# A graph network's second edge ranking moved from a stage of its own into the edge-score loop of the first layer

## The chip, the cores and the metric

The kernel runs on one core of a Trainium2 chip. The metric is the device time of one execution, in microseconds (us). Engines: PE is TensorE (matrix products; PEld its weight loads), DVE is VectorE, ACT is ScalarE, POOL is GpSimd, SP is SyncE, which here only issues DMAs. Each engine runs its own instruction stream in order; streams meet at semaphores.

## What is computed

Two layers, each a graph network and then a feed-forward network, on 3,125 nodes of 256 values and 53,125 edges sorted by destination. The parts that matter here, in short:

```python
# layer 0, graph: scores of the edges, softmax over each destination, weighted sum
h  = LN(x) @ Wn.T + bn
a  = leaky_relu(sum((h[src] + edge_attr @ We.T + be) * attn), 0.01)
x += relu(segment_sum(h[src] * softmax_by_dst(a), dst))
x += experts0(LN(x))                     # layer 0, feed-forward, 8 experts, top 2
# layer 1, graph: a second aggregation, now into the edges' SOURCE nodes
s   = LN(x) @ W
x += relu(batchnorm(segment_sum(edge_weight * s[dst], src) + bias))
...                                      # layer 1, feed-forward, with a third edge list
```

The second aggregation sums into `src`, by which the edges are not sorted. The kernel therefore ranks the edges by source: it computes for every edge the slot it has in an order by source tile (128 nodes), each tile padded to whole blocks of 6 x 128 slots. It then scatters one record per edge (destination, lane of the source, weight) to those slots in DRAM.

## The kernel before

The edges stand as 128 partitions x 416 chunks; the nodes are 25 tiles of 128. `build_kernel` emits blocks one after the other. Each block is a program for every engine, and the next begins when all engines have finished it. The blocks that matter, in order:

1. setup, layer norm and projection of layer 0, and `emit_sort_edges` (the third edge list's ranks; PE, VectorE and ScalarE).
2. **`emit_edge_scores`** (tiles `es_...`). A loop of 8 turns with two pieces each makes 16 pieces of 26 chunks. SP loads for a piece the transposed edge attributes `es_ea` (1,664 KB) and the source lanes `es_lane` (832 KB) into one of two buffers, once `read` says that the piece two before is done with. PE multiplies 26 f32 columns (L389, each counted in `step`), then makes 78 products with the one-hot lanes (L394; the last one counts `mm`). VectorE builds the one-hot lanes (L359, `hot`), waits for `mm`, and picks, reduces and adds the scores (L363 to L369), then counts `read`. POOL issues 176 scatters of the third edge list's records (L967). They are paced by single events: before each, `pace` waits for a count of `step` on PE.
3. `emit_aggregate` "a0": the first aggregation.
4. **`emit_rank_edges`** (tiles `se_...`), the stage that the change removes. POOL fills a record array with the values for empty slots (L1015 to L1018), and SP writes it to DRAM (L1010). VectorE makes a one-hot of all edges against all 25 source tiles (L1049). Then, per tile, PE makes two products over 416 columns (L1025: rank within a chunk, L1026: counts per chunk), and VectorE turns them into positions (L1053 to L1070). VectorE lets PE go on to the next tile with `tile_read`. L1072 to L1084 put the positions into `rece` and the tiles' ends into `eranges`.
5. layer norm and projection "l1", the gate, and `emit_experts` "f0". There POOL scatters the rest of the third list's records and, with `rece`, the 416 chunks of the second aggregation.
6. the second aggregation "a1" and the rest.

The wait that keeps PE and VectorE together in a tile of the ranking is this:

```python
with pe.Fori(0, NT) as t:
    pe.wait_ge(tile_read, t + 1)
    ...matmul(psr...); matmul(pst...).then_inc(ranked, 1)
# VectorE, per tile:
v.wait_ge(ranked, t + 1)
...scan, subtract, add (reads psr, pst)
v.drain().then_inc(tile_read, 1)
...multiply by the one-hot, add to pos and blocks
```

## Time and profile before

| what | us |
|---|---|
| median of 3 runs (3980.2 to 3986.33) | 3983.19 |
| the profiled execution | 3978.59 |
| its span, first to last instruction | 3976.6 |
| PE busy in the span | 2652.6 (67%) |
| VectorE busy | 1509.7 (38%) |
| ScalarE busy | 759.2 (19%) |
| POOL busy | 1882.4 (47%) |
| mean granted TensorE clock, share of full speed | 0.708 |

The profiled execution is one run on the chip. The shares are averages over stages that follow each other, and each stage has an engine of its own that sets its length. So the table tells what the whole is made of, and not what an edit in one stage is worth. A timeline row gives the start, the duration, engine, line and operation, output <- inputs and, in brackets, the idle time before it with what ended it. `x52` on such a row means that so many equal instructions were merged. An f32 product of PE runs as two passes, so the 26 columns of L389 are 52 records. A name with q (SPq, DVEq) is the engine's sequencer or queue.

### The profile page before, as it was taken

Reading aid. Unit: us, or ns where it says so; the run is one execution under the profiler, and the core shown is the slowest. Engines: PE = TensorE matmul, PEld = TensorE weight load, DVE = VectorE, ACT = ScalarE, POOL = GpSimd, SP = SyncE. Lnnn points to the kernel's source line nnn. Section 1 sums busy time; section 2 is a strip of 40 time slices with the busy share of each in tenths; the row PEclk is TensorE's granted clock in tenths of the full one; section 3 lists DMA queues with packets and bytes.
Section 4 is the critical chain, followed back from the end, with each engine's and each line's share of the span. In section 5 each row is a group of like instructions: output and inputs, shape, how many; then the busy total and the mean of one; then the engine's idle time right before and its main releaser. Section 6 shows DMA issues by size and latency. Waiting matters only on the chain. (4 is left out here: it accounts for less than half of the span.)

```text
span 3976.6 us, 46896 instructions
## 1 busy us (share of the span) xinstructions
PE 2652.6 (67%) x10550; PEld 1812.6 (46%) x10551; DVE 1509.7 (38%) x3668; ACT 759.2 (19%) x2605; POOL 1882.4 (47%) x1926
## 2 busy tenths in 40 slices
PE   3259886566666661389999999577776663989810
PEld 2135776333333330266676777333333343666600
DVE  5864112656666548622222222322222224001075
ACT  0136000232222220122222222111111111222200
POOL 0000664556565650056666666166666620666602
PEclk9555555666666665589999999766666665999955
DMA  2012442222232330010000000133333311111001
GB/s 71 26 44 65 149 160 104 69 76 79 75 80 75 80 76 13 0 32 11 12 12 12 12 13 1 60 90 89 91 89 91 90 44 26 18 14 19 8 36 35
DMA packets 125070, 213.67 MB, mean 54 GB/s; under 512 B 56130, under 2 KB 83095, under 8 KB 122711
## 3 DMA queue, kind: packets, MB, share of 16 engines
q0 software_dynamic: 75808, 125.28, 12.8%
q1 hardware_dynamic: 49206, 87.79, 6.5%
q8 instruction: 18, 0.29, 0.0%
q14 instruction: 38, 0.30, 0.0%
HBM read 197.42 MB, written 15.52 MB: 54 GB/s over the span
## 5 line engine op out<-in xcount | busy, mean ns | idle before, releaser
L503 POOL DMA_INDIRECT a0rows<-table,a0idx x462 | 472.4, 1022 | 349.6 <-ACT a0idx L488 235.3
L967 POOL DMA_INDIRECT records<-k_recg x288 | 287.4, 998 | 724.5 <-ACTq L306 366.6
L503 POOL DMA_INDIRECT a1rows<-table,a1idx x444 | 420.4, 947 | 316.8 <-ACT a1idx L488 172.1
L533 PE MATMUL a1ps<-a1rows,a1w 128*128 128x256 f32 x888 | 414.0, 590 | 195.3 <-DMA a1rows<-table,a1idx 135.3
L533 PE MATMUL a0ps<-a0rows,a0w 128*128 128x257 f32 x924 | 437.5, 614 | 154.2 <-ACT a0w L703 93.0
L967 POOL DMA_INDIRECT erecords<-k_rece x416 | 404.3, 972 | 209.0 <-issue 98.1
L795 PE MATMUL f0up<-k_xnT,f0w 128*128 x1280 | 380.3, 453 | 54.4 <-ACT f0hid L827 30.6
L1396 POOL DMA_INDIRECT gt_land<-table_gat,gt_source x281 | 266.0, 947 | 293.5 <-DVEq L1425 144.1
L533 PEld LDWEIGHTS a0ps<-a0rows,a0w 128*128 128x128 f32 x924 | 239.0, 292 | 348.5 <-issue 161.9
L533 PEld LDWEIGHTS a1ps<-a1rows,a1w 128*128 128x128 f32 x888 | 209.1, 274 | 400.2 <-issue 283.9
L805 PE MATMUL f0dn<-f0w,f0hid 128*128 128x256 f32 x1600 | 357.8, 380 | 11.4 <-issue 10.7
L805 PEld LDWEIGHTS f0dn<-f0w,f0hid 128*128 128x128 f32 x1600 | 303.4, 190 | 57.5 <-issue 16.9
L795 PEld LDWEIGHTS f0up<-k_xnT,f0w 128*128 128x128 f32 x1280 | 243.5, 196 | 187.6 <-issue 54.4
L746 DVE SCALAR_TENSOR_TENSOR k_x<-f0dn,k_gate,k_x 128x256 f32 (+1 forms) x200 | 87.0, 479 | 507.8 <-PE f0dn L805 312.4
L827 ACT ACTIVATE f0hid<-f0up,f0b1now 128x384 f32<-128x384 f32 (+1 forms) x320 | 168.0, 527 | 526.1 <-PE f0up L795 351.0
L572 DVE TENSOR_SCALAR a1w<-k_iota,k_elane,k_eweight 128x128 f32<-128x128 f32 x444 | 145.9, 366 | 267.3 <-PE a1ps L533 167.9
L1623 PE MATMUL f1up<-k_xnT,gt_arena 128*128 x640 | 190.5, 454 | 27.7 <-DVE gt_arena L1440 13.5
L1633 PE MATMUL f1dn<-gt_arena 128*128 128x256 f32 x800 | 189.3, 388 | 26.3 <-issue 22.9
L389 PE MATMUL es_ps<-k_we_attn,es_ea 128*128 128x1 f32 x832 | 180.7, 349 | 20.6 <-DMA es_lane<-lane_row 14.2
L488 ACT COPY a1idx<-k_esource 128x1 int32 x444 | 82.8, 191 | 580.4 <-PE a1ps L533 369.8
L389 PEld LDWEIGHTS es_ps<-k_we_attn,es_ea 128*128 128x128 f32 x832 | 180.0, 331 | 21.6 <-DMA es_lane<-lane_row 14.4
L703 ACT ACTIVATE a0w<-a0nb,k_score 128x128 f32 x462 | 143.5, 388 | 233.2 <-DVE a0nb L640 186.8
(389 smaller groups left out, 3115.2 us busy)
## 6 DMA issues: line engine op xcount, KB each, us to landing
es_ea<-in_eaT SPq DMA_DIRECT2D x16, 1664.0 KB
es_lane<-lane_row SPq DMA_DIRECT2D x16, 832.0 KB
so_rowl<-glane_row SPq DMA_DIRECT2D x32, 256.0 KB
a0rows<-table,a0idx POOLq DMA_INDIRECT x462
a1rows<-table,a1idx POOLq DMA_INDIRECT x444
erecords<-k_rece POOLq DMA_INDIRECT x416
table<-k_tbl SPq DMA_DIRECT2D x10, 650.0 KB, 3.4
records<-k_recg POOLq DMA_INDIRECT x288
```

Source lines behind the costliest of these rows:

```text
L389: nc.tensor.matmul(ps[i][:, 2, c:c + 1], ea[:, i, c * P:(c + 1) * P], S.we_attn[:, 0:1], start=True, stop=True).then_inc(step, 1)
L503: pool.indirect_dma_start(rows[:, i, 0:TW], None, table, bass.IndirectOffsetOnAxis(ap=idx[:, i:i + 1], axis=0)).then_inc(gathered[i], 16)
L533: nc.tensor.matmul(sum_of(t), w[:, i, :], rows[:, i, 0:width], start=False, stop=False).then_inc(agg_done, 1)
L572: nc.vector.tensor_scalar(w[:, i, :], S.iota[:, 0:P], S.elane[:, bass.ds(c + i, 1)], S.eweight[:, bass.ds(c + i, 1)], ALU.is_equal, ALU.mu ...
L703: nc.scalar.activation(w[:, i, :], nb[:, bass.ds(g % RING, 1), i, :].rearrange("p a n -> p (a n)"), ACT.Exp, bias=S.score[:, bass.ds(c + i ...
L795: ins = nc.tensor.matmul(up[q % 2][:, 0:size], w1[:, k, m * P:(m + 1) * P], S.xnT[:, k, bass.ds(g * (U * P) + a * P, size)], start=(k == 0 ...
L805: ins = nc.tensor.matmul(down[j][:, 0:D], hid[half][:, k, (j - a) * P:(j - a + 1) * P], w2[:, k, :], start=(k == 0), stop=(k == KH - 1))
L827: nc.scalar.activation(hid[half][:, m, :], up[q % 2][:, 0:(b - a) * P], ACT.Gelu, bias=bias_now[:, m:m + 1]).then_inc(hid_ready, 1)
L967: pool.indirect_dma_start(self.rec_dram, bass.IndirectOffsetOnAxis(ap=self.rec[:, c + 1, 0:1], axis=0), self.rec[:, c + 1, 1:R], None).the ...
L1396: pool.indirect_dma_start(land[:, j, :], None, S.table_gat, bass.IndirectOffsetOnAxis(ap=source[:, j:j + 1], axis=0)).then_inc(gathered[la ...
L1623: ins = nc.tensor.matmul(up[q % 2][:, 0:size], w1[:, k, m * P:(m + 1) * P], S.xnT[:, k, bass.ds(g * (U * P) + a * P, size)], start=(k == 0 ...
L1633: ins = nc.tensor.matmul(down[j][:, 0:D], hid[half][:, k, (j - a) * P:(j - a + 1) * P], w2[:, k, :], start=(k == 0), stop=(k == KH - 1))
```

## The change

The block `emit_rank_edges` is gone, and with it its call in front of "l1". `emit_edge_scores` gets its work:

- **Start of the block.** POOL's three memsets of the empty records come before its scatters (now into `erec_sb`, which is free until the scattered records are read back). SP waits for them and issues the 855 KB write to DRAM ahead of its first loads. VectorE makes the 25-tile one-hot (now `tile_hot`) before its loop, and PE waits for that (`hots`) before anything else. The two loads of the node numbers and two integer steps are gone, and four other short steps come behind the one-hot, since setup has left the same values in `S.srct`, `S.dstf` and `S.src`.
- **The loop.** Each turn of two pieces takes three tiles: 24 in 8 turns. PE does a tile's two products ahead of piece 0, one ahead of piece 1, and one between piece 1's f32 columns and its one-hot products. VectorE does one tile behind piece 0's one-hot and two behind piece 1's, both ahead of its wait for `mm`.
- **After the loop.** Tile 24, then the steps that write `eranges` and `rece`, ahead of the score's last steps.

The pacing of the scatters is as before. `rece` now lives with the edges' tiles, and the first table's tiles are given up before the sort, to make room. (The tables of setup, `emit_aggregate` and the experts are not touched.)

```diff
--- before.py
+++ after.py
@@ -311,12 +311,25 @@
...
+        pos, incl, part, zero = (sb(n, [P, NC], F32) for n in ("pos", "incl", "part", "zero"))
+        posi, lanei = sb("posi", [P, NC], I32), sb("lanei", [P, NC], I32)
+        tile_hot = sb("tilehot", [P, NT, NC], BF16)
+        trib, onesb = sb("trib", [P, P], BF16), sb("onesb", [P, P], BF16)
+        blocks, base, cnt = (sb(n, [P, 1], F32) for n in ("blocks", "base", "cnt"))
+        starts, under = sb("starts", [P, KB], F32), sb("under", [P, KB], F32)
+        row = sb("row", [P, NT + 1], F32)
         ps = [ctx.enter_context(nc.psum_tensor(f"es_ps{i}", [P, 3, 512], F32)) for i in range(2)]
+        psr = ctx.enter_context(nc.psum_tensor("es_psr", [P, 512], F32))
+        pst = ctx.enter_context(nc.psum_tensor("es_pst", [P, 512], F32))
+        hots, ranked, tile_read, filled, emptied = (sem("es_" + n) for n in ("hots", "rank", "tread", "fill", "empty"))
+        GB = BG * P
         block = ctx.enter_context(nc.Block())
         lane_row = S.lane_row.rearrange("(a n) -> a n", a=1)
...
         @block.sync
         def _(sp):
+            sp.wait_ge(filled, 1)
+            sp.dma_start(rec_dram.rearrange("(p c) r -> p c r", p=P), S.erec_sb[:]).then_inc(emptied, 16)
             with sp.Fori(0, NPIECE // 2) as o:
                 for i in range(2):
                     sp.wait_ge(read, 2 * o + i + 1)
@@ -325,10 +338,14 @@
...
+            sp.wait_ge(emptied, 16)
             scatter.finish(sp)
 
         @block.gpsimd
         def _(pool):
+            nc.gpsimd.memset(S.erec_sb[:, :, 0:1], 0)
+            nc.gpsimd.memset(S.erec_sb[:, :, 2:3], 0)
+            nc.gpsimd.memset(S.erec_sb[:, :, 1:2], 2 * P).then_inc(filled, 1)
...
@@ -353,11 +370,52 @@
...
+
+            v.sem_inc(tile_read, 1)
+            nc.vector.tensor_copy(trib[:], S.tri[:])
+            nc.vector.tensor_copy(onesb[:], S.ones[:, 0:P])
+            nc.vector.memset(zero[:], 0.0)
+            nc.vector.memset(pos[:], 0.0)
+            nc.vector.memset(blocks[:], 0.0)
+            nc.vector.memset(row[:], 0.0)
+            nc.vector.tensor_scalar(starts[:], S.iota[:, 0:KB], float(GB), None, ALU.mult)
+            nc.vector.tensor_tensor(tile_hot[:], S.srct[:, 0:NC].unsqueeze(1).to_broadcast([P, NT, NC]),
+                                    S.iota[:, 0:NT].unsqueeze(2).to_broadcast([P, NT, NC]), ALU.is_equal)
+            v.drain().then_inc(hots, 1)
+            nc.vector.tensor_scalar(lanei[:], S.src[:, 0:NC], P - 1, None, ALU.bitwise_and)
+            nc.vector.tensor_copy(rec[:, 1:NC + 1, 1], S.dstf[:, 0:NC])
+            nc.vector.tensor_copy(rec[:, 1:NC + 1, 3].bitcast(F32), S.ew[:, 0:NC])
+            v.drain()
+            nc.vector.tensor_copy(rec[:, 1:NC + 1, 2], lanei[:])
+
+            def rank_tile(t):
+                nc.vector.tensor_scalar(base[:], blocks[:], float(GB), None, ALU.mult)
+                v.wait_ge(ranked, t + 1)
+                nc.vector.tensor_tensor_scan(incl[:], pst[:, 0:NC], zero[:], 0.0, ALU.add, ALU.add)
+                v.drain()
+                nc.vector.tensor_tensor(part[:], incl[:], pst[:, 0:NC], ALU.subtract)
+                nc.vector.tensor_scalar(under[:], starts[:], incl[:, NC - 1:NC], None, ALU.is_lt)
+                v.drain()
+                nc.vector.tensor_tensor(part[:], part[:], psr[:, 0:NC], ALU.add)
+                nc.vector.tensor_reduce(cnt[:], under[:], AX.X, ALU.add)
+                v.drain().then_inc(tile_read, 1)
+                nc.vector.scalar_tensor_tensor(part[:], part[:], base[:, 0:1], tile_hot[:, bass.ds(t, 1), :].rearrange("p a c -> p (a c)"),
+                                               ALU.add, ALU.mult)
+                nc.vector.tensor_scalar(cnt[:], cnt[:], 1.0, None, ALU.max)
+                v.drain()
+                nc.vector.tensor_tensor(pos[:], pos[:], part[:], ALU.add)
+                nc.vector.tensor_tensor(blocks[:], blocks[:], cnt[:], ALU.add)
+                v.drain()
+                nc.vector.tensor_copy(row[:, bass.ds(t + 1, 1)], blocks[:])
+
             with v.Fori(0, NPIECE // 2) as o:
                 for i in range(2):
                     v.wait_ge(arrived[i], 32 * o + 32)
                     nc.vector.tensor_scalar(onehot[:, i, :], lane[:, i, :], S.lane[:, 0:1], None, ALU.is_equal
                                             ).then_inc(hot, 1)
+                    rank_tile(o * 3 + i)
+                    if i == 1:
+                        rank_tile(o * 3 + 2)
                     v.wait_ge(mm, 2 * o + i + 1)
...
@@ -369,6 +427,22 @@
...
                     v.drain().then_inc(read, 1)
+            with v.Fori(NT - 1, NT) as t:
+                rank_tile(t)
+            v.drain()
+            nc.vector.tensor_copy(S.eranges[:], row[:])
+            nc.vector.tensor_copy(posi[:], pos[:])
+            v.drain()
+            nc.vector.tensor_scalar(lanei[:], posi[:], P - 1, None, ALU.bitwise_and)
+            v.drain()
+            nc.vector.tensor_scalar(posi[:], posi[:], 7, None, ALU.logical_shift_right)
+            nc.vector.tensor_copy(part[:], lanei[:])
+            v.drain()
+            nc.vector.tensor_copy(pos[:], posi[:])
+            v.drain()
+            nc.vector.scalar_tensor_tensor(part[:], part[:], float(ES), pos[:], ALU.mult, ALU.add)
+            v.drain()
+            nc.vector.tensor_copy(rec[:, 1:NC + 1, 0], part[:])
...
@@ -380,14 +454,24 @@
...
         def _(pe):
+            def rank_tile(t):
+                pe.wait_ge(tile_read, t + 1)
+                counts = tile_hot[:, bass.ds(t, 1), :].rearrange("p a c -> p (a c)")
+                nc.tensor.matmul(psr[:, 0:NC], trib[:], counts, start=True, stop=True)
+                nc.tensor.matmul(pst[:, 0:NC], onesb[:], counts, start=True, stop=True).then_inc(ranked, 1)
+
             pe.wait_ge(split, 1)
+            pe.wait_ge(hots, 1)
             with pe.Fori(0, NPIECE // 2) as o:
                 for i in range(2):
+                    rank_tile(o * 3 + i)
                     pe.wait_ge(read, 2 * o + i + 1)
                     pe.wait_ge(arrived[i], 32 * o + 32)
                     for c in range(PIECE):
                         nc.tensor.matmul(ps[i][:, 2, c:c + 1], ea[:, i, c * P:(c + 1) * P], S.we_attn[:, 0:1],
                                          start=True, stop=True).then_inc(step, 1)
+                    if i == 1:
+                        rank_tile(o * 3 + 2)
                     pe.wait_ge(hot, 2 * o + i + 1)
                     for c in range(PIECE):
...
@@ -395,6 +479,8 @@
...
                         ins.then_inc(step if c < PIECE - 1 else mm, 1)
+            with pe.Fori(NT - 1, NT) as t:
+                rank_tile(t)
...
@@ -1691,37 +1668,35 @@
...
+        rece = sb_edges("rece", [P, NC + 1, 4], I32)
...
-            emit_layernorm_project(nc, S, "l0", S.w_aug, D + 1, False, rows_and_score, table, S.table_sb)
+            with ExitStack() as inner:
+                S.table_sb = sb("tbl0", [P, NT, TW], F32, inner)
+                S.w_aug = sb("w_aug", [P, KD, D + 4], F32, inner)
+                S.bn_row = sb("bn_row", [P, D], F32, inner)
+                emit_setup(nc, S, A)
+
...
+                emit_layernorm_project(nc, S, "l0", S.w_aug, D + 1, False, rows_and_score, table, S.table_sb)
             emit_sort_edges(nc, S, A)
-            emit_edge_scores(nc, S, A, Scatter(nc, S, "sa", recg, rec_dram, 0, EARLY))
+            emit_edge_scores(nc, S, A, Scatter(nc, S, "sa", recg, rec_dram, 0, EARLY), rece, erec_dram)
         emit_aggregate(nc, S, "a0", table, True)
...
         with ExitStack() as stage:
...
-            emit_rank_edges(nc, S, "se", NC, BG, A["dst_pc"][:, 0:NC], A["src_pc"][:, 0:NC], S.ew[:, 0:NC], ES, rece, erec_dram,
-                            S.eranges)
...
```

The deleted function is the one printed above.

On **PE**, the body of the edge-score loop before:

```order
L384 ISA
L387 ISA
L389 MATMUL es_ps<-k_we_attn,es_ea 128x1 x26
L394 MATMUL es_ps<-es_parts,es_hot 128x25 x78
L386 REGISTER_ALU
L389 MATMUL es_ps<-k_we_attn,es_ea 128x1 x26
L394 MATMUL es_ps<-es_parts,es_hot 128x25 x78
L384 REGISTER_ALU
L384 COMPARE_AND_BRANCH
```

and its second half (piece 1) now:

```order
L458 REGISTER_ALU
L460 ISA
L460 MATMUL es_psr<-es_tilehot,es_trib 128x416
L461 MATMUL es_pst<-es_tilehot,es_onesb 128x416
L468 REGISTER_ALU
L471 MATMUL es_ps<-k_we_attn,es_ea 128x1 x26
L458 REGISTER_ALU
L460 ISA
L460 MATMUL es_psr<-es_tilehot,es_trib 128x416
L461 MATMUL es_pst<-es_tilehot,es_onesb 128x416
L478 MATMUL es_ps<-es_parts,es_hot 128x25 x78
```

Two products of 416 columns stand ahead of the piece's f32 columns, two more between these and the 78 one-hot products; each pair waits for `tile_read` (the row L460 ISA carries that wait).

On **VectorE**, piece 1 of a turn before:

```order
L359 TENSOR_SCALAR es_hot<-es_lane,k_lane 128x3328 [waits es_in1]
L361 REGISTER_ALU
L363 ISA [waits es_mm]
L363 TENSOR_TENSOR es_picked<-es_ps,k_src_tile 128x650
L367 ISA
L367 TENSOR_REDUCE k_score<-es_picked 128x26
L369 TENSOR_TENSOR k_score<-k_score,es_ps 128x26
```

Now the same piece begins with the first of two ranking tiles:

```order
L414 TENSOR_SCALAR es_hot<-es_lane,k_lane 128x3328 [waits es_in1]
L392 TENSOR_SCALAR es_base<-es_blocks 128x1
L393 REGISTER_ALU
L394 SCALAR_TENSOR_TENSOR es_incl<-es_pst,es_zero 128x416 [waits es_rank]
L396 TENSOR_TENSOR es_part<-es_incl,es_pst 128x416
L397 TENSOR_SCALAR es_under<-es_starts,es_incl 128x71
```

and after the second of them comes what stood there:

```order
L404 TENSOR_SCALAR es_cnt<-es_cnt 128x1
L406 TENSOR_TENSOR es_pos<-es_pos,es_part 128x416
L407 TENSOR_TENSOR es_blocks<-es_blocks,es_cnt 128x1
L409 ISA
L409 COPY es_row<-es_blocks 128x1
L419 REGISTER_ALU
L421 ISA [waits es_mm]
L421 TENSOR_TENSOR es_picked<-es_ps,k_src_tile 128x650
L425 ISA
L425 TENSOR_REDUCE k_score<-es_picked 128x26
L427 TENSOR_TENSOR k_score<-k_score,es_ps 128x26
```

Between the one-hot (`es_hot`) and the wait for `es_mm` there are now two tiles of the ranking with a wait of their own each (`es_rank`). The three score steps, behind which `read` frees the piece's buffers for SP, come after them.

## Rows read from the trace of the kernel before

**Rows 1.** Busy time by stretch: ranking stage, edge scores, a stretch of the first experts

```profile
core 0: us, PE busy (x) PEld busy (x) DVE busy (x) ACT busy (x) POOL busy (x), PEclk, DMA share, GB/s
1492.98:1638.35 145.37, 21.82 (x50) 3.30 (x50) 122.98 (x297) 0.00 (x0) 2.35 (x3) 0.50 0.02 9
404.15:673.88 269.73, 223.52 (x2080) 218.61 (x2080) 48.32 (x68) 0.00 (x0) 169.49 (x168) 0.50 0.38 139
1725.00:1750.00 25.00, 25.00 (x109) 20.31 (x108) 5.28 (x13) 4.94 (x10) 15.80 (x18) 1.00 0.02 1
```

**Rows 2.** Timeline (start, duration, engine, line), start of the ranking stage

```profile
1492.99 0.85 POOL L1015 MEMSET se_empty<- 128x570 int32 x1 [9.90 <-POOLq L1660]
1493.12 2.29 DVE L1032 CAST se_trib<-k_tri 128x128 bf16<-128x128 f32 x1 [1.36 <-PEq L1660]
...
1495.36 0.33 SPq L1010 DMA_DIRECT2D erecords<-se_empty  x1
...
1496.40 0.36 DVE L1040 TENSOR_SCALAR se_tile<-se_dst 128x416 int32<-128x416 int32 x1
...
1498.85 10.99 DVE L1049 TENSOR_TENSOR se_hot<-se_tilef,k_iota 128x10400 bf16<-128x10400 f32 x1
```

**Rows 3.** Timeline, two late tiles of the ranking and its end

```profile
1620.09 0.15 DVE L1053 TENSOR_SCALAR se_base<-se_blocks 128x1 f32<-128x1 f32 x1 [0.22 <-issue]
...
1623.02 0.52 PE L1025 MATMUL se_psr<-se_hot,se_trib 128*128 x1 [4.08 <-DVEq L1062]
...
1623.34 0.55 PE L1026 MATMUL se_pst<-se_hot,se_onesb 128*128 x1
...
1625.04 0.15 DVE L1053 TENSOR_SCALAR se_base<-se_blocks 128x1 f32<-128x1 f32 x1 [0.22 <-issue]
...
1634.81 0.18 DVE L1072 CAST k_eranges<-se_row 128x26 int32<-128x26 f32 x1
...
1637.49 0.53 DVE L1084 CAST k_rece<-se_part 128x416 int32<-128x416 f32 x1
1638.35 0.38 SPq L1736 DMA_DIRECT2D k_wg<-in_Wg  x1
```

**Rows 4.** DMA issues of the ranking stage: KB each, median us to landing

```profile
erecords<-se_empty SPq DMA_DIRECT2D x1, 855.0 KB, 3.7
```

**Rows 5.** Instruction groups in the edge scores (busy, mean ns, idle before)

```profile
L389 PE MATMUL es_ps<-k_we_attn,es_ea 128*128 128x1 f32 x832 | 180.7, 349 | 20.6 <-DMA es_lane<-lane_row 14.2 <-issue 5.7
...
L394 PE MATMUL es_ps<-es_parts,es_hot 128*128 128x25 bf16 x1248 | 46.1, 182 | 35.7 <-issue 35.6
...
L363 DVE TENSOR_TENSOR es_picked<-es_ps,k_src_tile 128x650 f32<-128x650 f32 x16 | 13.4, 835 | 212.9 <-remote 110.4 <-PE es_ps L394 62.5 <-issue 40.0
```

**Rows 6.** Timeline of PE in the edge scores, pieces 0, 14 and 15

```profile
418.00 0.27 PE L394 MATMUL es_ps<-es_parts,es_hot 128*128 128x25 bf16 x4 [0.43 <-issue]
...
641.24 11.25 PE L389 MATMUL es_ps<-k_we_attn,es_ea 128*128 128x1 f32 x52 [0.21 <-issue]
...
667.54 2.24 PE L394 MATMUL es_ps<-es_parts,es_hot 128*128 128x25 bf16 x78
```

**Rows 7.** Timeline of SP's queue in the edge scores

```profile
394.26 0.35 SPq L324 DMA_DIRECT2D es_ea<-in_eaT  x1
...
427.67 0.33 SPq L324 DMA_DIRECT2D es_ea<-in_eaT  x1
```

**Rows 8.** Timeline of VectorE in the edge scores, start and piece 0

```profile
404.13 1.09 DVE L359 TENSOR_SCALAR es_hot<-es_lane,k_lane 128x3328 bf16<-128x3328 bf16 x1 [10.20 <-DMA es_lane<-lane_row]
425.38 0.83 DVE L363 TENSOR_TENSOR es_picked<-es_ps,k_src_tile 128x650 f32<-128x650 f32 x1 [20.17 <-remote]
```

**Rows 9.** Timeline, the edge scores' end on VectorE

```profile
669.94 0.83 DVE L363 TENSOR_TENSOR es_picked<-es_ps,k_src_tile 128x650 f32<-128x650 f32 x1 [7.39 <-PE es_ps L394]
...
673.29 0.59 DVE L377 TENSOR_TENSOR k_score<-k_score,es_picked 128x416 f32<-128x416 f32 x1
```

**Rows 10.** Timeline of POOL in the edge scores, one scatter

```profile
397.58 0.96 POOL L967 DMA_INDIRECT records<-k_recg  x1 [0.30 <-issue]
```

More of the change, by code:

```diff
@@ L296, in _, with emit_edge_scores @@
                              start=True, stop=True).then_inc(small, 1)
-def emit_edge_scores(nc, S, A, scatter):
+def emit_edge_scores(nc, S, A, scatter, rec, rec_dram):
     sem = S.sem
@@ L1699, in build_kernel @@
         with ExitStack() as stage:
-            S.table_sb = sb("tbl0", [P, NT, TW], F32, stage)
-            S.w_aug = sb("w_aug", [P, KD, D + 4], F32, stage)
-            S.bn_row = sb("bn_row", [P, D], F32, stage)
             S.we_attn, S.bias_attn = sb("we_attn", [P, 1], F32, stage), sb("bias_attn", [P, 1], F32, stage)
@@ L1705, in build_kernel, with rows_and_score @@
             S.src_tile = sb("src_tile", [P, NC, NT], BF16, stage)
[L1706 to L1713 removed]
+            with ExitStack() as inner:
[3 more added lines that the diff above has]
+                emit_setup(nc, S, A)
+                def rows_and_score(v, o, i, ps):
+                    nc.vector.tensor_tensor(S.table_sb[:, bass.ds(o * U + i, 1), 0:D], ps[:, 0:D].unsqueeze(1),
+                                            S.bn_row[:].unsqueeze(1), ALU.add)
+                    nc.vector.tensor_copy(S.hs[:, bass.ds(o * U + i, 1)], ps[:, D:D + 1])
+                emit_layernorm_project(nc, S, "l0", S.w_aug, D + 1, False, rows_and_score, table, S.table_sb)
             emit_sort_edges(nc, S, A)
[L1715 removed]
+            emit_edge_scores(nc, S, A, Scatter(nc, S, "sa", recg, rec_dram, 0, EARLY), rece, erec_dram)
         emit_aggregate(nc, S, "a0", table, True)
@@ L1720, in build_kernel @@
         with ExitStack() as stage:
-            rece = sb("rece", [P, NC + 1, 4], I32, stage)
-            emit_rank_edges(nc, S, "se", NC, BG, A["dst_pc"][:, 0:NC], A["src_pc"][:, 0:NC], S.ew[:, 0:NC], ES, rece, erec_dram,
-                            S.eranges)
             S.xnT = sb("xnT0", [P, KD, NP], F32, stage)
```

104 lines of the change are left out of this document (removed).

## The prediction, made before the changed kernel ran

> **What bounds the kernel now.** I first took the busy time by stretch, to see what the removed stage and the stage that takes its work are made of. The ranking stage lasts 145.37 us [rows 1]. In it VectorE is busy 122.98 us, PE 21.82, POOL 2.35, and DMA has a share of 0.02: a chain on VectorE, with nothing beside it. The edge scores last 269.73 us [rows 1]. There PE is busy 223.52 us and VectorE 48.32.
>
> The groups of instructions tell who waits for whom there [rows 5]. VectorE stands idle for 212.9 us ahead of its pick (L363), mostly for PE. PE waits for a load once, 14.2 us at the start, and never for VectorE. Its other idle time, 35.6 us, lies between the one-hot products (L394), ended by nothing the profile shows. So PE sets this stage, VectorE has room in it, and the ranking is VectorE's work. The question is what of it comes to lie on PE's path, and what at the ends.
>
> From the timelines: one tile of the ranking takes 1625.04 - 1620.09 = 4.95 us [rows 3], all on VectorE; PE's two products hide in it. A piece of the edge scores takes (667.54 + 2.24 - 404.15) / 16 = 16.6 us on average [rows 6, 8]: 11.25 us of f32 columns [rows 6] and some 5 of one-hot products and their gaps.
>
> **Removed.** The stage runs from its first instruction at 1492.98 to the next stage's first load at 1638.35 [rows 1, 3]. All engines begin and end it together, and nothing of another stage is in it, so the whole of it goes: **-145.4 us**. What follows needs nothing prepared there but `rece` and `eranges`, which are used later.
>
> **Added at the start.** PE can't begin before VectorE's one-hot over 25 tiles. In the ranking stage that one-hot ended at 1498.85 + 10.99 = 1509.84, 16.85 us behind the block's first instruction at 1492.99 [rows 2]. The steps from 1496.40 to 1498.85 (2.45 us) [rows 2] are gone or stand behind it now, so 14.4 us are left. The first casts took 2.29 us beside POOL's memsets [rows 2]; the memsets come along, and I let them cost the same. With about 1 us for the score parts that this block makes first, and PE's pair of products, the f32 columns begin some 16.3 us into the block. They began about 11 us in: the score parts ended on VectorE at 404.13 - 10.20 = 393.93 [rows 8], so this block began near 393. This gives **+5.3 us**. The other way in is SP's. Its first load waits for the memsets (1495.36 - 1492.99 = 2.4 us [rows 2]), where it now goes out at 394.26 [rows 7], about 1.2 us into the block, and for one issue more: some 1.8 us later in all. It goes out behind the 855 KB write, which took 3.7 us to land [rows 4]. At worst, that is 5.5 us: the two ways cost the same, and only one counts. Bounds: 3, if the casts don't wait, and 9, if write and load slow each other.
>
> **Added in the loop, PE.** 24 pairs of 416-column products, one of them counted above, 23 left. Alone, a pair keeps PE busy for 21.82 / 25 = 0.87 us [rows 1]. In a stream it takes twice the distance of its two starts, 2 x (1623.34 - 1623.02) = 0.64 us [rows 3]. The pairs stand between other products, with one wait each, which lies between the two; I take 0.75: 23 x 0.75 = **+17.3 us**, bounds 14.7 and 20.0. The waits on `tile_read` should be met. VectorE gives it back 2.9 us after `ranked` (PE's next pair starts at 1623.02, the tile began at 1620.09 [rows 3]), and between pairs PE has either 11.25 us of f32 columns or some 5 us of one-hot products.
>
> **Added in the loop, VectorE: nothing, but with little left.** In a turn of two pieces it has two one-hots (1.09 us each [rows 8]), twice the pick and its followers (2.3 us from the pick at 425.38 to the load that it releases at 427.67 [rows 7, 8]) and three tiles of 4.95: 21.6 us against a turn of 2 x 16.6 + 3 x 0.75 = 35.4. The cover is PE, 13.8 us of it. In piece 0 of a turn, VectorE is done with its tile long before `mm`. In piece 1 the second tile can only begin when PE has finished the f32 columns, and its 4.95 us lie beside one-hot products that take 2.2 [rows 6] to 5. So `read` comes 0 to 2.7 us late there, and with it the load for two pieces on. A load took 9.9 us (394.26 to 404.13 [rows 7, 8]). A buffer's round, load 9.9 + piece 16.6 + 2.3, with 2.7 of lateness, is 31.5 against 35.4: about 4 us of room. If that cover went, each late microsecond would cost one.
>
> **Added at the end.** The last piece has no load beside it, and its one-hot products took only 2.24 us [rows 6]; tile 23 on VectorE is then late by 4.95 - 2.24 = 2.7. Tile 24 takes 4.95 more, since PE's pair for it is done by then. The steps that write `eranges` and `rece` take 1637.49 + 0.53 - 1634.81 = 3.2 [rows 3]. Sum **+10.9 us**, bounds 9 and 14. The score's last steps (to 673.88 [rows 9]) come behind that as before.
>
> **Gaps in the one-hot products.** 35.6 us of PE's idle time [rows 5] may shrink, since the pairs move these products later against the loads beside them, or grow, since each turn's code is longer. I take 0, with bounds of -15 and +20.
>
> **POOL.** 176 scatters at 0.96 + 0.30 = 1.26 us [rows 10] are 222 us, of a stage that grows to about 303. The three memsets delay it by 2.4 us, and the pacing holds it back anyway. Nothing.
>
> **Sum.** 3978.6 (the profiled execution) - 145.4 + 5.3 + 17.3 + 10.9 = 3866.7 us. The median of the runs lies 4.6 us above the profiled execution, so I forecast a median of **3871 us**, 2.8% faster. About 0.2%, 8 us, is what a measurement of this kernel can tell from no change.
>
> **Rivals.**
>
> *Late releases.* In piece 0 PE's one-hot products ended at 418.27, yet VectorE's pick began at 425.38 [rows 6, 8]: 7.1 us late, for a reason that the profile calls "remote", 110.4 us of such waits in 7 places [rows 5]. The timeline has this in 4 of 16 pieces. It costs little now. With a longer VectorE loop it may come in every turn: 7.1 + 1.5 of lateness on average - 4 of room = 4.6 us in each of 8 turns, 37 us: 3908. Against it: the ranking's own loop kept its 4.95 us with no such stall. The Trainium skill ("Runtime: NRT & Kernel Launch", Instruction fetch mechanics) says that a taken branch to code outside the instruction pages at hand makes the engine wait for a fetch. That speaks against longer loop bodies such as these; no row here shows a fetch, and its time would be this rival's.
>
> *A warm PE.* The stage runs at a granted clock of 0.50, 1.2 GHz, while PE is busy 223.52 of 269.73 us; in the experts 1.00 is granted [rows 1]. If the added wide products brought 1.00 here, the f32 columns would fall to half, 5.6 us less in 16 pieces, 90 us. POOL's scatters, 222 us from about 396 on, would then bound the stage about as tightly, and 88 us would be gained: 3866.7 - 88 + 4.6 = 3783. Against it: the ranking stage ran the very same products at 0.50 too [rows 1]. The Trainium skill ("TensorE: Matmul & The Clock Gate", Part 1) says that the clock is held down by default and that work on PE releases it. By this rule the busy edge scores should already be at 2.4 GHz; the row speaks against it, so I hold to the row.
>
> *Not hidden.* The ranking could stay a chain of its own, PE and VectorE waiting for each other tile by tile. Then 24 x 4.95 = 119 us stand in place of 17.3: 3973, no measurable change or barely faster.
>
> *Slower.* The late release falls on every wait of VectorE, five in a turn: 21.6 + 5 x 7.1 = 57.1 us a turn against 35.4, 8 x 21.7 = 174 us: 4045. It decides from the cover of 13.8 us plus the gain, 112 / 8 = 14 us a turn: 28 us of stalls, four of five waits. Before, one comes in two turns.
>
> **Chances.** Forecast 0.78 (on its own 3849 to 3900), late releases 0.12, warm PE 0.03, not hidden 0.03, slower 0.04. Faster by over 0.2% are the first three and a third of the fourth: 0.94; within 0.2%: 0.02; slower: 0.04. The low end takes all lower bounds: 3866.7 - 2.3 - 2.6 - 1.9 - 15 + 4.6 = 3849, rounded down to 3846 for the spread of the runs. The high end takes in the late releases, 3908, with 4 us of the same spread: 3912. That leaves out one in ten.
>
> **What would show it.** Right: no stretch between "a0" and "l1"; edge scores of about 303 us, PE pairs near 0.75 us apart, no wait of PE for `tile_read` or for a load inside the loop, first f32 columns about 5 us later, some 11 us on VectorE behind the last pick's PE work. Wrong: PE idle ahead of f32 columns for a DMA in many pieces (late releases), a granted clock over 0.5 in the stage, or VectorE tiles longer than 4.95 us.

## The result, and the profile after

The changed kernel takes 3861.53 us (median of 4 runs, 3854.0 to 3866.02). The one before takes 3983.47 us beside it (4 runs, 3980.2 to 3986.33). The ratio is 0.9692, with a 95% interval of 0.9672 to 0.9712. That is 3.1% faster, 9.5 us less than forecast and inside the range. The profiled execution took 3854.00 us, with a span of 3851.9.

First the busy time by stretch of the changed kernel. The first row is the whole of the edge scores, which is to be held against the second of [rows 1]. The second is a stretch of 14 us, nearly all of it PE's one-hot products of piece 0.

```profile
core 0: us, PE busy (x) PEld busy (x) DVE busy (x) ACT busy (x) POOL busy (x), PEclk, DMA share, GB/s
409.64:701.91 292.27, 237.02 (x2129) 223.82 (x2127) 153.53 (x354) 0.00 (x0) 177.90 (x173) 0.50 0.35 125
420.00:434.00 14.00, 4.71 (x83) 3.66 (x84) 0.00 (x0) 0.00 (x0) 8.61 (x9) 0.50 0.02 2
```

VectorE was busy 48.32 us in the stage and is now busy 153.53. The stage grew from 269.73 us to 292.27, and the granted clock stayed at 0.50.

Then PE's groups in the stage, the ones of [rows 5] and the new pairs (L460, L461; their 25th, for tile 24, stands in rows of its own):

```profile
L471 PE MATMUL es_ps<-k_we_attn,es_ea 128*128 128x1 f32 x832 | 178.1, 349 | 2.7 <-issue 2.7
L478 PE MATMUL es_ps<-es_parts,es_hot 128*128 128x25 bf16 x1248 | 46.5, 183 | 37.0 <-issue 36.0 <-DVEq L401 0.9
...
L461 PE MATMUL es_pst<-es_tilehot,es_onesb 128*128 x24 | 13.2, 552 | 0.2 <-issue 0.2
L460 PE MATMUL es_psr<-es_tilehot,es_trib 128*128 x24 | 12.3, 513 | 20.9 <-DVEq L384 19.2 <-issue 1.1 <-DVEq L401 0.7
```

PE never waits for a load. It waits 19.2 us once for VectorE's 25-tile one-hot (L384 is the drain behind it). In the loop the profile puts 1.6 us down to `tile_read` (L401).

The start, in the timeline:

```profile
392.50 0.85 POOL L346 MEMSET k_erec<- 128x570 int32 x1 [366.12 <-POOLq L1076]
392.54 2.35 DVE L362 CAST es_parts<-k_hs 128x25 bf16<-128x25 f32 x1 [0.37 <-PEq L1076]
...
394.88 0.32 SPq L332 DMA_DIRECT2D erecords<-k_erec  x1
...
396.21 0.35 SPq L337 DMA_DIRECT2D es_ea<-in_eaT  x1
...
397.51 10.98 DVE L382 TENSOR_TENSOR es_tilehot<-k_srct,k_iota 128x10400 bf16<-128x10400 f32 x1
...
397.89 11.43 POOL L1053 DMA_INDIRECT records<-k_recg  x1 [0.30 <-issue]
...
408.97 0.53 PE L460 MATMUL es_psr<-es_tilehot,es_trib 128*128 x1 [19.17 <-DVEq L384]
...
409.63 2.05 POOL L1053 DMA_INDIRECT records<-k_recg  x1 [0.30 <-issue]
409.64 1.71 PE L471 MATMUL es_ps<-k_we_attn,es_ea 128*128 128x1 f32 x8
```

The f32 columns begin at 409.64, where they began at 404.15. The whole block begins at times that are up to 3 us apart from run to run, so where runs are compared below I count from VectorE's first step in it. That step stood here before:

```profile
392.72 0.18 DVE L345 CAST es_parts<-k_hs 128x25 bf16<-128x25 f32 x1 [0.37 <-PEq L1099]
```

So the columns begin 17.09 us into the block, where they began 11.43 us into it. One row is a surprise: a scatter of 11.43 us beside the one-hot, where scatters take 0.96 [rows 10].

A pair of products at the head of a piece:

```profile
433.72 0.51 PE L460 MATMUL es_psr<-es_tilehot,es_trib 128*128 x1
434.02 0.55 PE L461 MATMUL es_pst<-es_tilehot,es_onesb 128*128 x1
434.37 2.77 PE L471 MATMUL es_ps<-k_we_attn,es_ea 128*128 128x1 f32 x13
```

It costs 434.37 - 433.72 = 0.65 us. The stage's end:

```profile
685.17 2.28 PE L478 MATMUL es_ps<-es_parts,es_hot 128*128 128x25 bf16 x78
...
690.12 0.83 DVE L421 TENSOR_TENSOR es_picked<-es_ps,k_src_tile 128x650 f32<-128x650 f32 x1
...
692.54 0.15 DVE L392 TENSOR_SCALAR es_base<-es_blocks 128x1 f32<-128x1 f32 x1 [0.35 <-issue]
...
699.98 0.54 DVE L445 CAST k_rece<-es_part 128x416 int32<-128x416 f32 x1
...
701.32 0.59 DVE L451 TENSOR_TENSOR k_score<-k_score,es_picked 128x416 f32<-128x416 f32 x1
```

The last pick comes 690.12 - 687.45 = 2.67 us behind PE, tile 24 begins at 692.54, and `rece` is written by 700.5. Where the ranking stage stood, the last step of "a0" is now followed directly by the first load of "l1":

```profile
1514.35 0.42 DVE L740 TENSOR_TENSOR k_x<-k_x,a0relu 128x256 f32<-128x256 f32 x1
...
1516.01 0.39 SPq L1711 DMA_DIRECT2D k_wg<-in_Wg  x1
```

The whole by stages, each length read from the timelines (us). "Loop" goes from the first f32 column to the last one-hot product's end, "tail" from there to the start of the score's last step. "a0" begins at that step and ends at the start of its last addition, and "l1" begins with its first statistics (L83). "The rest" ends at the start of the last addition to `k_x`, some 8 us before the end of the span.

| | before | after |
|---|---|---|
| f32 columns begin | 404.15 | 409.64 |
| loop | 265.6 | 277.8 |
| tail | 3.51 | 13.87 |
| "a0" | 818.0 | 813.0 |
| end of "a0" to "l1" | 150.77 | 5.43 |
| "l1" and the experts f0 | 857.5 | 861.8 |
| second layer norm and a1 | 803.8 | 801.8 |
| the rest | 665.5 | 660.8 |

The ranking's place gave back 145.3 us, and the edge scores took 5.49 + 12.19 + 10.36 = 28.0. The other four stages together are 7.4 us shorter.

### The profile page after: what moved, and what is told of

It is laid out like the page before. It is cut to its first block and busy times, and to the rows that moved or that the text cites. A ratio compares the mean times of both kernels' runs of the same rounds, so it can differ in the third digit from the quotient of the medians.

```text
span 3851.9 us, 46754 instructions
## 1 busy us (share of the span) xinstructions
PE 2660.5 (69%) x10550; PEld 1816.4 (47%) x10551; DVE 1510.2 (39%) x3666; ACT 759.3 (20%) x2605; POOL 1889.8 (49%) x1926
## 3 DMA queue, kind: packets, MB, share of 16 engines
q0 software_dynamic: 75808, 125.28, 13.1%
## 5 line engine op out<-in xcount | busy, mean ns | idle before, releaser
L619 PE MATMUL a1ps<-a1rows,a1w 128*128 128x256 f32 x888 | 435.5, 616 | 173.2 <-DMA a1rows<-table,a1idx 115.9
L619 PE MATMUL a0ps<-a0rows,a0w 128*128 128x257 f32 x924 | 428.3, 602 | 153.6 <-ACT a0w L789 71.4
L1053 POOL DMA_INDIRECT records<-k_recg x288 | 301.0, 1045 | 226.1 <-POOLq L959 74.2
L1610 PEld LDWEIGHTS f1dn<-gt_arena 128*128 128x128 f32 x800 | 152.8, 193 | 62.1 <-issue 42.3
```

The lines of the kernel that those rows point to most:

```text
L619: nc.tensor.matmul(sum_of(t), w[:, i, :], rows[:, i, 0:width], start=False, stop=False).then_inc(agg_done, 1)
L1053: pool.indirect_dma_start(self.rec_dram, bass.IndirectOffsetOnAxis(ap=self.rec[:, c + 1, 0:1], axis=0), self.rec[:, c + 1, 1:R], None).the ...
L1610: ins = nc.tensor.matmul(down[j][:, 0:D], hid[half][:, k, (j - a) * P:(j - a + 1) * P], w2[:, k, :], start=(k == 0), stop=(k == KH - 1))
```

## The experiments

All are edits of the changed kernel. The kernel before took 4007.76 us beside e1 to e4, 4027.11 beside e5, e7, e8 and e9, and 3975.05 (median of 9 runs) beside e10, e11, e12 and e14. Only e11 and e12 were run five times, the others once. So a total says little to a few us, and I compare the lengths of stretches in the traces. The loop and the tail are those of the table above. Even these vary: the loop is 277.8 us in the changed kernel, 276.9 in the same kernel run again (e12) and 281.6 in e4, whose loop has the same instructions. I take up to 5 us of loop as no difference.

### Is VectorE's cover real, and what does a PE pair cost?

Two edits lengthen VectorE's tile by further scans, one doubles PE's pair, and one sends the 855 KB write behind the loads:

```diff
@@ e1: PE's rank_tile @@
+                nc.tensor.matmul(pst[:, 0:NC], onesb[:], counts, start=True, stop=True)
+                nc.tensor.matmul(psr[:, 0:NC], trib[:], counts, start=True, stop=True)
@@ e2 (range(3)) and e3 (range(7)): VectorE's rank_tile @@
-                nc.vector.tensor_tensor_scan(incl[:], pst[:, 0:NC], zero[:], 0.0, ALU.add, ALU.add)
-                v.drain()
+                for again in range(7):
+                    nc.vector.tensor_tensor_scan(incl[:], pst[:, 0:NC], zero[:], 0.0, ALU.add, ALU.add)
+                    v.drain()
@@ e4: SP @@
-            sp.wait_ge(filled, 1)
-            sp.dma_start(rec_dram.rearrange("(p c) r -> p c r", p=P), S.erec_sb[:]).then_inc(emptied, 16)
             with sp.Fori(0, NPIECE // 2) as o:
...
+            sp.wait_ge(filled, 1)
+            sp.dma_start(rec_dram.rearrange("(p c) r -> p c r", p=P), S.erec_sb[:]).then_inc(emptied, 16)
```

> PE makes each tile's two products of the ranking twice over (same result, one signal). My theory: the pairs lie on PE's path at 0.65 us each, so the loop of the edge scores, 277.8 us from the first f32 column to the last one-hot product, grows by 24 x 0.65 = 15.6 us, to 293. Rival, that PE's gaps between one-hot products absorb them (PE waits there anyway): under 5 us more.

> VectorE repeats a tile's scan twice more, 2.2 us more per tile, 6.6 in a turn. My theory: VectorE has room (21.6 us of work in a turn of 34.7), and only what stands behind PE's f32 columns counts: PE waits some 1 us a turn for tile_read, about 8 us in the loop, and 4.4 us come at the end (tile 23 and 24): the stage grows by 11 us, to about 303.5 from the first f32 column to the last score step. Rival, late releases (each microsecond of VectorE counts one for one): 8 x 6.6 = 53 us.

> The same with six scans more, 6.6 us per tile and 19.8 in a turn: VectorE has 41.4 us of work against a turn of 34.7. My theory: cover used up, PE waits for tile_read ahead of f32 columns in each turn, a turn grows to about 40, 8 x 5.3 = 42 us in the loop, 13 at the end, 55 in all. Rival, late releases one for one: 158 us. Rival, a VectorE that is free anyway: 13 us, at the end only.

> SP issues the 855 KB write of the empty records behind the loop's loads and not ahead of them (the wait for POOL's memsets goes with it), VectorE's one-hot over 25 tiles stays. My theory: the one-hot sets the start, the first f32 column stays at 409.6 us and the time is unchanged. Rival, the write and the loads behind it set the start: first f32 column 3 to 5 us earlier.

| | time | f32 begin | loop | tail |
|---|---|---|---|---|
| e4, write behind the loads | 3892.82 | 409.1 | 281.6 | 13.9 |
| e1, pairs twice | 3888.47 | 409.0 | 287.2 | 13.9 |
| e2, two scans more | 3909.49 | 409.9 | 281.3 | 18.9 |
| e3, six scans more | 3970.48 | 408.7 | 330.7 | 27.9 |

e4 is the changed kernel but for its write, and it ran beside the other three, so it is the row to compare with here. Two scans more add some 6.6 us of VectorE work to each turn. PE does wait 9.0 us for `tile_read` in the loop (4.2 in e4), about what was expected, but the loop did not grow by it: PE's idle time ahead of the f32 columns went from 3.0 us to nothing, and against the changed kernel's 277.8 the loop is 3.5 us longer, within its spread. Only the tail, where nothing covers, clearly grows, by 5.0. Six more (19.8 us a turn) lengthen the loop by 49 us, and PE now waits for the tile, as its group in e3 shows:

```profile
L461 PE MATMUL es_psr<-es_tilehot,es_trib 128*128 x24 | 12.5, 520 | 94.7 <-DVEq L402 75.5 <-DVEq L384 19.2
```

49 us in 8 turns are 6.1 a turn, so 19.8 - 6.1 = 13.7 us of it were covered (13.1 if one takes e12's loop to compare with). The prediction's cover was 13.8. It is real, and a late release does not cost one for one.

In e1 the second pair should add 23 x 0.65 = 15 us. The loop grew by 5.5 (10.3 against e12), less than the theory and more than the rival said, while the one-hot products' idle time fell from 38.8 us (e4) to 30.2:

```profile
L480 PE MATMUL es_ps<-es_parts,es_hot 128*128 128x25 bf16 x1248 | 45.0, 183 | 30.2 <-issue 30.1
```

PE time spent on wide products is partly won back from these gaps. e4 did not move the start: 17.09 us into the block, as in the changed kernel. So VectorE's one-hot sets it. But e4 did not send the loads out sooner either. The first goes out 3.7 us into the block in both, since SP also waits for `read`, which VectorE counts behind its first steps, and the first of these now takes 2.35 us beside POOL's memsets and took 0.18 before.

### Where the one-hot products' gaps and the late picks come from

Three edits: e9 loads both buffers in full once and then only 128 columns for each piece, so the pieces behind the first two are scored from stale data. e10 issues 8 scatters in the stage and not 176, the others in the experts. e14 paces the scatters by the f32 columns alone.

```diff
@@ e9: SP @@
-                    sp.dma_start(ea[:, i, :], A["eaT"][:, bass.ds(col, PIECE * P)]).then_inc(arrived[i], 16)
-                    sp.dma_start(lane[:, i, :], lane_row[:, bass.ds(col, PIECE * P)].to_broadcast([P, PIECE * P])
+                    sp.dma_start(ea[:, i, 0:P], A["eaT"][:, bass.ds(col, P)]).then_inc(arrived[i], 16)
+                    sp.dma_start(lane[:, i, 0:P], lane_row[:, bass.ds(col, P)].to_broadcast([P, P])
@@ e10 @@
-EARLY = 176
+EARLY = 8
@@ e14: POOL and PE @@
-            STEPS = 2 * PIECE - 1
+            STEPS = PIECE
...
-                        ins.then_inc(step if c < PIECE - 1 else mm, 1)
+                    ins.then_inc(mm, 1)
```

> Both buffers of the edge-score loop are loaded in full once, and each piece then loads only its first 128 columns and lanes (64 and 32 KB for 1,664 and 832); the scores of the later pieces are computed from stale data. Theory: the idle time between PE's one-hot products (36 us in the changed kernel, 35.6 before) comes from the loads that move beside them, so it falls under 8 us and the loop from 277.8 to about 250 us; what was saved on pairs by shrinking gaps is then the reason why the loop grew by less than its pairs. Rival, that the gaps are the engine's own (a loop body too long for its code supply): they stay above 25 us.

> Only 8 of the 176 scatters stay beside the edge scores, 168 go to the first experts, where POOL then has them on top. Theory after the run with small loads: PE's gaps between one-hot products come from the scatters that POOL issues beside them, so they fall from some 36 us to under 5 and the loop to about 240 us; the whole gets slower, since POOL's scatters set the length of the first experts (168 x 1.26 = 212 us more for POOL there). Rival, that the gaps are PE's own code supply: over 25 us of them stay.

> PE's one-hot products no longer count in step, by which POOL paces its scatters; only the f32 columns do (26 events a piece for 51). Theory: the gaps come from the scatters and not from the signals, so they stay within 25 to 45 us and the loop within 4 us. Rival, that PE is held by signalling to POOL: the gaps fall by more than half.

e9, busy time by stretch, and its one-hot products' group in the listing by line:

```profile
420.00:680.00 260.00, 218.72 (x1985) 208.04 (x1984) 129.72 (x293) 0.00 (x0) 168.82 (x164) 0.50 0.04 6
```

```profile
L484 PE MATMUL es_ps<-es_parts,es_hot 128*128 128x25 bf16 x1248 | 45.1, 183 | 31.1 <-issue 30.8
```

The changed kernel has 138 GB/s and a PE busy for 218.33 us in that window. Without the loads' traffic (6 GB/s) PE is as idle as before. The theory was wrong, loads are not the cause.

e10, the same two views:

```profile
409.20:654.30 245.10, 226.03 (x2129) 218.30 (x2127) 152.61 (x353) 0.00 (x0) 6.72 (x7) 0.50 0.39 149
```

```profile
L478 PE MATMUL es_ps<-es_parts,es_hot 128*128 128x25 bf16 x1248 | 36.1, 182 | 0.0
```

Without 168 of the scatters the gaps are gone, all of them, and the loop is 230.65 us long. That is 47.2 us less than in the changed kernel, 0.28 us for each scatter on average. The picks are now on time as well. They come 0.17 us behind `mm` in piece 0 of every turn and 2.68 in piece 1, which is what the prediction's working gives (4.95 - 2.28). In the changed kernel three pieces have picks clearly later than that (6.66, 3.93 and 9.36 us), with the code just as long. The last of them in the timeline (PE's last one-hot product had started at 584.35, and took 0.18):

```profile
593.89 0.84 DVE L421 TENSOR_TENSOR es_picked<-es_ps,k_src_tile 128x650 f32<-128x650 f32 x1 [7.77 <-remote]
```

The whole of e10 is slower all the same, 4034.83 us: "l1" and the experts take 1085 us in place of 862, since POOL sets the length there (224 us for 168 scatters, 1.33 each). A scatter beside the edge scores costs 0.28 us, and in the experts 1.33.

e14 is a miss. Fewer signals should have changed little. The gaps doubled, the loop came to 309.9 us, and the total to 3891.24:

```profile
L478 PE MATMUL es_ps<-es_parts,es_hot 128*128 128x25 bf16 x1248 | 50.7, 183 | 70.3 <-issue 70.2
```

No pick is late in it, with all 176 scatters issued. So both gaps and late picks depend on where the pacing lets scatters fall, and not on their number alone. Counted in the timelines, 45 scatters of the changed kernel start between a piece's last f32 column and its last one-hot product, 31 of them less than 0.4 us behind the one before. In e14 it is 55, and all 55 of them so. Why a scatter holds up PE's small products and hardly its f32 columns stays open. The runs do not separate POOL's work of issuing from the packets that it sends, either.

The fetching of code, which the prediction named, can be seen in the traces. These are the instruction queues' packets in the changed kernel's loop, from 409 to 690 (count, MB, share):

```profile
q8 instruction: 3, 0.05, 0.1%
q14 instruction: 4, 0.03, 0.0%
```

Seven fetches stand against gaps in 14 of the 16 pieces, so they can't be what PE waits for in most of them. In e10, without gaps, there are four.

### The parts of the change by themselves

```diff
@@ e8: no interleaving, all 25 tiles behind the loop (PE and VectorE) @@
-                    rank_tile(o * 3 + i)
-                    if i == 1:
-                        rank_tile(o * 3 + 2)
...
-            with v.Fori(NT - 1, NT) as t:
+            with v.Fori(0, NT) as t:
@@ e5: the second pair in the middle of piece 1's f32 columns (PE) @@
                     for c in range(PIECE):
+                        if i == 1 and c == HALF:
+                            rank_tile(o * 3 + 2)
...
-                    if i == 1:
-                        rank_tile(o * 3 + 2)
@@ e7: no 25-tile one-hot; read the one that setup has left (PE and VectorE) @@
-            nc.vector.tensor_tensor(tile_hot[:], S.srct[:, 0:NC].unsqueeze(1).to_broadcast([P, NT, NC]),
-                                    S.iota[:, 0:NT].unsqueeze(2).to_broadcast([P, NT, NC]), ALU.is_equal)
...
-                counts = tile_hot[:, bass.ds(t, 1), :].rearrange("p a c -> p (a c)")
+                counts = S.src_tile[:, :, bass.ds(t, 1)].rearrange("p c a -> p (c a)")
```

> No stage of its own, but no interleaving either: all 25 tiles are ranked behind the loop of the edge scores, in the same block. Theory: the loop falls back to about 266 us (no pairs), and 25 x 4.95 = 124 us stand behind it, so the tail from the last one-hot product to the last score step is about 130 us for 13.9, and the whole is some 104 us slower than the changed kernel: nearly all of the gain is the interleaving. Rival, that ending a stage (its barriers, loads and memsets) was worth much: less than 90 us slower.

> The third tile's pair of a turn stands in the middle of piece 1's f32 columns, not behind them. Theory: VectorE then makes that tile beside f32 columns; the last pick is no longer 2.7 us late and PE's waits for tile_read behind the loop body (1.4 us) go, so the stage shrinks by some 4 us. Rival: VectorE's late picks (4 to 9 us behind the end of the products, in 4 of 16 pieces) now hold PE in the middle of its columns, and the loop grows by up to 4 x 7 = 28 us.

> The 25-tile one-hot is not made; PE and VectorE read the same numbers, one in 25 elements, from the table that setup has made for the scores. Theory: the start is then set by the write and the loads behind it, the first f32 column comes 2 to 4 us earlier (near 406), the scatter that took 11.4 us beside the one-hot takes about 1, and the pairs keep their 0.65 us if PE reads its moving operand as fast at that stride. Rival: the strided read costs PE, and pairs of 1.3 us add 15 us to the loop.

**e8** took 4012.61 us, against 4027.11 of the kernel before. Its windows, the loop and what comes behind it:

```profile
410.01:688.93 278.92, 226.30 (x2081) 218.50 (x2082) 46.86 (x65) 0.00 (x0) 175.31 (x174) 0.50 0.36 132
688.93:819.90 130.97, 21.72 (x51) 3.21 (x50) 109.69 (x290) 0.00 (x0) 0.00 (x0) 0.50 0.00 0
```

The tail is 130.3 us, where the changed kernel has 13.87: the interleaving alone is worth 116.5 us of it. The loop was expected to fall to the 266 us of before and did not, though its PE work did: 45.8 us of gaps stand in the one-hot products, where the kernel before has 35.7 and the changed one 37.0. The gaps have two parts that only show when piece 0 is taken by itself. Piece 0 and then pieces 1 to 15, before:

```profile
L394 PE MATMUL es_ps<-es_parts,es_hot 128*128 128x25 bf16 x78 | 2.6, 182 | 0.4 <-issue 0.4
...
L394 PE MATMUL es_ps<-es_parts,es_hot 128*128 128x25 bf16 x1170 | 43.6, 182 | 35.2 <-issue 35.1
```

and in the changed kernel:

```profile
L478 PE MATMUL es_ps<-es_parts,es_hot 128*128 128x25 bf16 x78 | 4.0, 182 | 9.3 <-issue 9.3
...
L478 PE MATMUL es_ps<-es_parts,es_hot 128*128 128x25 bf16 x1170 | 42.5, 183 | 27.7 <-issue 26.7 <-DVEq L401 0.9
```

Piece 0's gaps rose by 8.9 us. They are 9.1 us in e8 too, which makes the 25-tile one-hot but has no pairs in the loop, and 2.5 in e7 below, which has pairs but no such one-hot. They come with the scatters that the one-hot held back, and that POOL then issues one behind the other. In the other 15 pieces the gaps are 35.2 us before and 36.8 in e8, without pairs; 27.7 (28.2 in e12) with them; and 21.1 in e1, with twice as many. This is what wide products put into this loop win back.

**e5** is a miss, its rival came true: the loop came to 289.9 us, 8 to 13 more than with the pair behind the columns (276.9 to 281.6), though the tail fell to 11.4. PE's pair now waits for a VectorE that has not yet given back the tile before:

```profile
L460 PE MATMUL es_psr<-es_tilehot,es_trib 128*128 x24 | 12.4, 519 | 34.7 <-DVEq L384 19.2 <-DVEq L401 13.6 <-issue 1.9
```

**e7** takes the one-hot out of PE's way, and the f32 columns begin only 2.3 us earlier (14.82 us into the block). Here the loads, behind the write, end last (7.7 <-DMA):

```profile
L468 PE MATMUL es_ps<-k_we_attn,es_ea 128*128 128x1 f32 x832 | 177.2, 349 | 7.7 <-DMA es_lane<-lane_row 7.7
...
L458 PE MATMUL es_pst<-k_src_tile,es_onesb 128*128 x23 | 20.6, 897 | 0.0
L457 PE MATMUL es_psr<-k_src_tile,es_trib 128*128 x23 | 20.2, 877 | 2.1 <-DVEq L398 1.8 <-issue 0.2
```

A product takes 877 ns and not 513, since its moving columns now stand 25 values apart. The loop is 275.9 us all the same, as the gaps in the one-hot products are 24.1 us here and not 37.0. Half of that difference lies in piece 0. And beside this start, with no one-hot on VectorE, no scatter is long:

```profile
398.08 1.16 POOL L1050 DMA_INDIRECT records<-k_recg  x1 [0.30 <-issue]
```

### A version that beats both

e11 puts together e7 (no one-hot), e4 (write behind the loads) and tile 0 ahead of the loop, so that none is left behind it. e12 is the changed kernel again, unaltered, on the same chip.

```diff
+            with pe.Fori(0, 1) as t:
+                rank_tile(t)
             with pe.Fori(0, NPIECE // 2) as o:
                 for i in range(2):
-                    rank_tile(o * 3 + i)
+                    if i == 1:
+                        rank_tile(o * 3 + 2)
...
-                    if i == 1:
-                        rank_tile(o * 3 + 2)
+                    rank_tile(o * 3 + 1 + 2 * i)
...
-            with pe.Fori(NT - 1, NT) as t:
-                rank_tile(t)
```

> Three edits together: no 25-tile one-hot (strided reads of the table that is there), the write of the empty records behind the loads, and tile 0 ranked ahead of the loop while the loads are under way, so that 24 tiles fill the loop and none is left behind it (piece 0 of a turn has its pair behind its f32 columns, piece 1 one ahead and one behind). Theory: first f32 column 3 to 5 us earlier (near 405), tail 10 us for 13.9, loop as before within 4 us: 7 to 12 us faster than the change, ratio to it 0.997 to 0.998. Rival: the strided pairs and the late tile in every piece give it back, no difference.

> The changed kernel unaltered, to be compared with the others of this call on the same chip. Theory: 0.969 of the kernel before, edge scores (first f32 column to last score step) 292 to 296 us, and the parts behind them vary by a few us from run to run with no cause in the change.

e11 takes 3843.51 us (5 runs, 3839.21 to 3851.32), ratio to the kernel before 0.9678 (0.9658 to 0.9699). e12 takes 3854.07 (5 runs, 3851.73 to 3859.82), ratio 0.9702 (0.9683 to 0.9722). The runs of the two don't overlap, barely (3851.32 against 3851.73), and the medians are 10.6 us apart; the two ratios' intervals touch. The profiled executions are 17.1 us apart. Of that, 6.9 stand in the edge scores, counted from VectorE's first step to the start of the last one (300.9 against 307.8): f32 columns 3.7 us sooner (13.41 us into the block, and 17.09), tail 4.3 shorter, loop 1.1 longer. For the rest, outside the edit, I give no cause. Moving the write alone brought the start nothing (e4), dropping the one-hot alone 2.3 us (e7), both 3.7.

## Why the prediction was right, point by point

- **Removed, -145.4.** Measured -145.3 (150.77 to 5.43). e8 shows that the gain is that of the interleaving: with the work merely moved, one run of each gives 14.5 us for the whole.
- **Start, +5.3.** Measured +5.5. The one-hot's way decided (e4), and the loads' way does as soon as the one-hot is gone (e7). That the two cost the same was wrong: counted within the block, the one-hot's way costs 5.7 us (11.43 to 17.09) and the loads' 3.4 (to 14.82 in e7).
- **PE in the loop, +17.3.** Measured +12.2 for the whole loop. This term was too high, by 5 us: the pair costs 0.65 and not 0.75, which makes 15.0. Then PE's f32 columns and their idle time fell by 2.6 and 3.7 (busy 180.7 to 178.1, idle ahead of them 6.4 to 2.7 without the first wait). The idle time ahead of the pairs (1.7) and the one-hot products (1.3 of gaps and 0.4 of busy time) took 1.7 each of this back.
- **VectorE in the loop, nothing.** Right. The loop stands 6.6 us more work a turn at no cost that can be told from its spread, and not 19.8 (e2, e3).
- **End, +10.9.** Measured +10.4, with the pick 2.67 us late for 2.7.
- **Gaps, 0.** The sum came out right (35.7 to 37.0), and that is luck: +8.9 us in piece 0 and -7.5 in the others happened to cancel. The causes named, loads beside them and the length of the code, were wrong: e9 takes the loads away and e10 keeps the code, and it is e10 that has no gaps. They come with POOL's scatters. With as many scatters, other kernels here have 22.1 us of gaps (e11) and 70.3 (e14).
- **POOL, nothing.** Wrong, though the sum does not show it. The one-hot held a scatter for 11.43 us, and POOL then issued its late ones back to back: 9 scatters in 14 us of window 420 to 434, with PE busy 4.71. Piece 0's one-hot products took 13.3 us there, where they took 3.0 before (5.4 in e7). This is the +8.9 us of the line above. The prediction asked only whether POOL would be done in time, and not what its scatters do to PE.
- **What is left over.** By the terms measured the profiled execution should be 117.3 us faster, by the forecast's 111.9; it is 124.6. So of the 12.7 us between forecast and profile, 5.4 stand in the terms, and the remaining 7 in stages that the change does not touch (-5.0, +4.2, -2.0, -4.7). e12, the same kernel again, has 816.2, 859.0, 802.1 and 663.5 us there, so lengths of this kind vary by some 3 us between equal programs. I give them no cause.

Of the rivals, *late releases* exist and cost nothing that the traces show: picks come up to 9.36 us late, and no f32 column waits for a load. The code supply is not what delays them: e10 has the same loops and no late pick, and the whole loop has seven fetches. The rule from the Trainium skill ("Runtime: NRT & Kernel Launch", Instruction fetch mechanics), by which a taken branch outside the pages at hand waits for a fetch, finds nothing here that it could explain. *A warm PE* did not come: the clock is 0.50 in the stage, with PE busy 237.02 of 292.27 us. The rule of the Trainium skill ("TensorE: Matmul & The Clock Gate", Part 1), that work on PE releases the clock, does not tell this stage's clock, not even when the one-hot products have no gaps (e10: 226.03 of 245.10 us, 0.50). *Not hidden* and *slower* did not happen either. Their price is e8's tail and e3's waits.

## What to carry to other kernels

A stage that is a chain on one engine can go into a loop that another engine sets, if the loop's turn leaves that engine room. Here the sum of instruction times per turn (21.6 of 35.4 us) told it well, and an experiment that lengthens the guest engine's work finds where the room ends. Ask for each handshake where the guest engine is at that moment: a pair moved by half a piece cost some 10 us. Idle time that the profile puts down to nothing may belong to an engine that the idle one never waits for, and leaving that engine's work out is the run that tells. And a sum of gaps that stays the same is no proof that nothing changed: take it by pieces.

## What the runs showed of the hardware

- **A scatter waits for a VectorE instruction.** POOL's scatter, begun 0.38 us behind the 10.98 us one-hot, took 11.43 us and ended 0.83 behind it. Without the one-hot it took 1.16 (e7), and before the change 0.96 beside the same loads [rows 10]. The Trainium skill ("SBUF — State Buffer", SBUF: two separate sides) says that a VectorE operation with two inputs in SBUF, once begun, keeps the port pair that it shares with GpSimd for its whole length against a GpSimd operation that reads SBUF; the trace agrees, 11.43 against 10.98 us, though no row names a port. VectorE is slowed beside POOL as well: its first cast took 2.35 us beside POOL's three memsets, which end 0.04 us before it, and 0.18 without them.
- **A scatter costs PE time though PE waits for nothing of POOL's.** 168 of them cost the loop 47.2 us, 0.28 each, nearly all in the 25-column products: 37.0 us of gaps and 10.4 of busy time (46.5 to 36.1). Where late scatters ran back to back, PE made the first 37 such products in 1.14 us (from 420.59) and then three to five at a time, 1.44 us apart (421.92, 423.36, 424.80):

```profile
424.80 0.24 PE L478 MATMUL es_ps<-es_parts,es_hot 128*128 128x25 bf16 x3 [1.18 <-issue]
425.50 0.18 PE L478 MATMUL es_ps<-es_parts,es_hot 128*128 128x25 bf16 x1 [0.46 <-issue]
```

- **Late picks are gone in both runs that changed the scatters**: e10, which takes them out, and e14, which keeps them all and paces them otherwise. So in these runs a late pick takes scatters, and scatters at certain places. How the one delays the other is open, and the kernel before was not run without scatters.
- **A moving operand read with a stride costs PE 1.7 times**: 877 against 513 ns for 416 bf16 columns, at the granted clock of 0.50, when they stand 50 bytes apart and not side by side (e7).
